# Routed experts in 21 blocks of 128 token slots instead of 14 of 256, with the shared expert's second half as jobs in the same buffers

## What is computed

```
probs = softmax(x @ gate_w.T)                       # 8 experts
routing_weights, selected = top_k(probs, 2)         # normalized to sum 1
out = (silu(x @ shared_gate.T) * (x @ shared_up.T)) @ shared_down.T      # width 704
y_e = (silu(x @ expert_gate[e].T) * (x @ expert_up[e].T)) @ expert_down[e].T   # width 352
out = out + sum over the two selected e of weight_e * y_e
```

## Time and profile before

| | us |
|---|---|
| median of 3 runs | 1053.2 (1052.33 to 1053.86) |
| the profiled execution | 1054.41 |
| its span | 1052.5 |
| mean granted clock of TensorE | 0.982 of 2.4 GHz |

### The profile page before, as it was taken

The page is one execution under the profiler, slowest core; times in us unless marked ns, Lnnn a source line. Parts: engine busy times, 40 slices in busy tenths (PEclk is TensorE's granted clock), DMA queues, the critical chain, the costliest instruction groups (busy, mean ns, idle before and its releaser), DMA issues.

```text
span 1052.5 us, 18925 instructions
## 1 busy us (share of the span) xinstructions
PE 993.0 (94%) x7782; PEld 863.8 (82%) x7782; DVE 540.2 (51%) x1163; ACT 486.8 (46%) x1176; POOL 254.4 (24%) x160
## 2 busy tenths in 40 slices
PE   5999999999999997889999999997897999999998
PEld 4999989899999996667777777775676999999986
DVE  6353535444444444556556556645283555555546
ACT  3351514233233434266666666664332566666631
POOL 1220211202020332020010001002046344434453
PEclk9999999999999998899999999998998999999999
DMA  5110741111010021121010011001047466666545
GB/s 174 62 60 21 237 123 61 42 39 60 21 61 21 21 101 59 50 85 47 21 31 21 12 31 30 12 2 61 31 146 258 187 238 230 234 234 244 195 166 163
DMA packets 41188, 102.50 MB, mean 97 GB/s; under 512 B 3488, under 2 KB 21136, under 8 KB 39184
## 3 DMA queue, kind: packets, MB, share of 16 engines
q1 hardware_dynamic: 38544, 93.97, 26.5%
q0 software_dynamic: 2560, 7.34, 2.1%
HBM read 79.28 MB, written 20.19 MB: 95 GB/s over the span
## 4 chain that ended last, share of the span: by engine, by line
PE 48%; DVE 6%; ACT 2%; POOL 1%; issue 1%; DMA 1%; SPq 0%; ACTq 0%; DVEq 0%
PE bank L444 13%; PE bank L446 12%; PE bank L445 12%; PE bank L641 3%; PE bank L658 3%; PE bank L608 1%; PE bank L759 1%; POOL slots L1831 1%; DVE rq L1397 1%; PE bank L668 1%; DVE kn L1410 0%; DVE yg L1611 0%; PE bank L532 0%; DMA sf<-moe 0%; DVE kT L1419 0%
## 5 line engine op out<-in xcount | busy, mean ns | idle before, releaser
L1736 POOL TENSOR_TENSOR E_lo<-F,E_hi 128x940 fp32r<-128x940 f32 (+1 forms) x28 | 79.9, 2855 | 115.9 <-ACT E_hi L858 115.9
L1018 ACT ACTIVATE ee<-bank 125x448 f32<-125x448 f32 x192 | 91.2, 548 | 23.2 <-PE bank L641 22.2
L444 PE MATMUL bank<-xT_hi,wqk_hi 128*128 128x448 f32 x256 | 96.0, 375 | 1.4 <-DVE xT_lo L1256 1.4
L444 PE MATMUL bank<-xgT_hi,E_hi 128*128 128x256 f32 (+1 forms) x336 | 95.2, 283 | 0.0
L446 PE MATMUL bank<-xgT_lo,E_hi 128*128 128x256 f32 (+1 forms) x336 | 94.7, 282 | 0.0
L445 PE MATMUL bank<-xgT_hi,E_lo 128*128 128x256 f32 (+1 forms) x336 | 94.3, 281 | 0.0
L446 PE MATMUL bank<-xT_lo,wqk_hi 128*128 128x448 f32 x256 | 93.8, 367 | 0.0
L445 PE MATMUL bank<-xT_hi,wqk_lo 128*128 128x448 f32 x256 | 93.8, 366 | 0.0
L444 PE MATMUL bank<-wkv_hi,ctx_hi 128*125 128x512 f32 x192 | 81.5, 424 | 9.6 <-DVE kn L1410 7.8
L1736 POOL TENSOR_TENSOR ctx_lo<-ctx_f,ctx_hi 128x500 fp32r<-128x500 f32 x24 | 29.9, 1246 | 216.1 <-ACT ctx_hi L858 216.1
L445 PE MATMUL bank<-wkv_hi,ctx_lo 128*125 128x512 f32 x192 | 77.1, 402 | 0.0
(11 more groups left out here) (333 smaller groups left out, 2616.2 us busy)
## 6 DMA issues: line engine op xcount, KB each, us to landing
F<-wexp SPq DMA_DIRECT2D x14, 2176.0 KB, 8.5
wqk_f<-wqk SPq DMA_DIRECT2D x16, 512.0 KB, 3.3
slots<-zt SPq DMA_DIRECT2D x1, 7168.0 KB, 29.2
xg<-slots SPq DMA_DIRECT2D x14, 512.0 KB, 3.8
slots_out<-yg SPq DMA_DIRECT2D x28, 256.0 KB, 2.1
sf<-moe SPq DMA_DIRECT2D x9, 768.0 KB
ctx_f<-ctx SPq DMA_DIRECT2D x24, 250.0 KB, 2.7
wv_f<-wv SPq DMA_DIRECT2D x8, 512.0 KB, 3.5
```

The lines of the kernel that those rows point to most:

```text
L444: e.matmul(out, a[0], b[0], start=first, stop=False)
L1018: e.activation(ee[(4 * n + r) % 8][:, :], SX[r][0:MS, 0:4 * T], ACT.Exp, scale=0.25).then_inc(*x_exped.did((n, r)))
L1736: return e.tensor_tensor(out, src, high.bitcast(F32), ALU.subtract)
```

## The change

- BS is 128, so there are 21 routed blocks. They run as jobs in the order s0, e0 to e20, s1, s2. A job s is two chunks of the shared expert's second half, whose weights (2 x 1536 columns) are loaded into the same F and split into the same E as an expert's.
- In a routed job the slots are stationary: 2 (gate, up) x 4 x 3 = 24 matmuls of 352 columns, the weights moving. silu x up comes out with slots on the partitions, so h is turned by 3 transposes into PSUM and split from there by ScalarE and VectorE (384 columns each). The downward product is 9 matmuls of 512 columns and is done during the next job, between or after that job's upward products. x is turned (4 transposes) one job ahead, with two xgT and four xg buffers.
- y is copied out of PSUM by VectorE instead of ScalarE. The low part of the downward piece is made half by VectorE, half by GpSimd (768 columns each).
- The weights come as two DMAs, upward (1408 KB) and downward (768 KB) part, each with a register load of the expert number before it and a semaphore of its own.
- A shared job's downward product sums its two chunks and is added to the output rows by VectorE tile by tile. The last additions of gathered rows: tokens 0 to 447 (additions 0 to 7) after the last split of h, then s2's four tiles, then additions 8 to 15.

The orders of the jobs, cut to their core:

```diff
-BS = 256
+BS = 128
+        jobs = [("s", 0)] + [("e", j) for j in range(NBLK)] + [("s", 1), ("s", 2)]
 # TensorE
+            def expert_up(j, a):
+                for k in range(KC):
+                    i = mm3(GU[u][:, 0:NI], at(xgT[j % 2], ALL, k, ALL), at(p, ALL, toks(k * 2 * NI + a * NI, NI)), k == 0, k == KC - 1)
+            def job_pe(k):
+                kind, j = jobs[k]
...
+                if kind == "e":
+                    expert_up(j, 0)
+                else:
+                    up_pe(1, 2 * j, 0)
+                if prev and prev[0] == "e":
+                    turn_h(prev[1])
+                elif prev and kind == "e":
+                    job_down(*prev)
+                if kind == "s":
+                    up_pe(1, 2 * j, 1)
+                    if k == 0:
+                        up_pe(1, 2 * j + 1, 0)
+                if nxt[0] == "e":
+                    turn_x(nxt[1])
+                if kind == "e":
+                    expert_up(j, 1)
+                if prev and (prev[0] == "e" or kind == "s"):
+                    job_down(*prev)
+                if kind == "s":
+                    if k:
+                        up_pe(1, 2 * j + 1, 0)
+                    up_pe(1, 2 * j + 1, 1)
 # ScalarE, routed job k (part_hi waits for the load's DMA, and for the last reader of E)
+                if kind == "e":
+                    part_hi(k + 1, 0)
+                    if nxt[0] == "e":
+                        part_hi(k + 1, 1)
+                if prev[0] == "e":
+                    ht_hi_act(prev[1])
...
+                if nxt[0] == "e":
+                    turned_hi(nxt[1])
+                if kind == "e":
...
+                    silu(("b", j), ("b", j, 0), (sg1 if j % 2 else sg[0])[:, 0:NI])
+                    if nxt[0] == "e":
+                        part_hi(k + 1, 2)
+                    part_hi(k, 3)
 # VectorE: part_low(k+1,0), ht_low, turned_low, product, part_low(k+1,2), part_low(k,3), y_out(prev)
 # VectorE at the end
+            for n in range(8):
+                add_back(n)
+            y_out(*jobs[-1])
+            for n in range(8, 16):
+                add_back(n)
 # SyncE (part_load(k, p) waits for the low parts of job k - 2 in the same buffer)
+            for k in range(len(jobs)):
+                if k:
+                    part_load(k + 1, 3)
+                part_load(k + 2, 0)
+                if k and jobs[k - 1][0] == "e":
+                    j = jobs[k - 1][1]
+                    w.wait_ge(*y_done["e", j])
+                    e.dma_start(y_d[j * BS:(j + 1) * BS, :], yg[j % 4][:, :]).then_inc(*yo_out[j % 4].did(j))
+                    xg_load(j + 4)
```

## The result

The changed kernel takes 1064.5 us, the median of 4 runs (1063.1 to 1068.1), beside 1053.2 before (1052.3 to 1053.9): ratio 1.0113, 95% interval 1.0086 to 1.0140. Forecast were 1043.7 and faster; it is 11.3 us slower, outside the range of 1020 to 1060. The profiled execution took 1063.1 at a span of 1061.0.

A forecast was written before the change was run, and what follows sets the result against it. TensorE bound the old expert stage; afterwards a loop through SyncE's order would, 2P = 10 + 7.3, 8.65 us per block. With head and tail the span is 1043; 1043 + 1.9 - 1.2 = 1043.7 us, range 1020 to 1060.

The forecast's parts named there:

- a ring through SyncE's wait for y: Expert stage: upward loads are issued only after SyncE's wait for y; the loop passes two jobs, 8.65 us per block.
- I take D+10 for the landing, F: Expert stage: upward weights of job k+3 land (F) 10 us after y of job k's turn is ready (D).
- by landing: Rival, expert stage: weights land at D+11.5, 9.4 us per block, 1057 us in all; chance 14%.
- the head: Before the routed blocks: TensorE's hole shrinks from 6.2 to 2 us without the slow clock; job 2 starts at 824.8.
- the tail: Kernel's end: last gathers wait for additions, last addition at 1039.6, span 1043; about 9 us over TensorE's own end.
- one of my two sums: Landing in the expert stage: by the queue D+9.6, by adding everything to the first issue D+10.2; x and y 1.7.
- F to D: Expert stage: from the weights' landing, ScalarE's 5.6, VectorE's 0.94 and the y copy's 0.69 give the next D at F+7.3.
- TensorE's price: Expert stage: 352-column matmuls at 0.159 us each, 6.7 us per new block, 141 instead of 190.7 us in all.
- Clock: Expert stage: clock stays 1.00; rival, gaps drop it to 1.2 GHz, 95 us more, 1138 us, chance 3%.
- Lock, GpSimd first: Rival, end of each job: GpSimd takes its 768 columns before VectorE, D 1.75 later, 9.5 per block, 1060 us; chance 10%.
- The busiest resource binds, 7.3: Rival, expert stage: loads land sooner or their wait is hidden, 7.3 us per block, 1020 us; chance 16%.
- All are near or above 6.7: Expert stage: ScalarE, VectorE, the VectorE-GpSimd lock and DMA each need near or over TensorE's 6.7 us per block.

The follow-up runs named there:

- experiment 3: Changed kernel with the upward load of job k+2 issued before SyncE's wait for y of job k-2: 1040.2 us, ratio 0.9861 to the kernel before.
- experiment 10: Changed kernel with each routed expert's downward load cut to a quarter of its columns from job 4 on, upward loads whole: 1048.7 us.
- experiments 7 and 12: Changed kernel, from block 4 on, with x loads cut to 64 of 512 columns (1065.4 us), or with y stores cut to 64 of 512 (1066.4 us).
- experiment 9: Experiment 3's kernel with GpSimd's pieces cut to 64 columns from job 4 on: 1036.8 us.
- experiment 8: Changed kernel with eight extra 512-column products on TensorE ahead of each routed job's wait for the low half of h: 1064.9 us.

## Why the prediction was wrong
The mechanism stood in the forecast: a ring through SyncE's wait for y, closed by the landing of the weights. Opening it alone gives back 24 us (experiment 3). **The step that failed is a size: "I take D+10 for the landing, F".** It measures 11.4, and the rival "by landing", D+11.5, given 14%, is what happened in the stage; its time, 1057, is still 7.5 short. By the 10.8 that the lag cost, the forecast would have been 1054.5, an estimate, inside its range: what carried it past 1060 lies in the head and the tail, in which the slow clock was put at nothing, and in 2.8 us around the span. The terms:
- SyncE's issues: first weight load at D+1.8, measured 1.9 to 2.5, mostly 1.9 to 2.0; upward load at about D+3.1. Right.
- From the upward issue to the landing I had 7.0, measured 8.3. The data were priced at 418 GB/s, read from a stretch of 1 us. Single stretches reach that here too (384 to 453), but the difference between loads gives 347 (experiment 10), by which the 2.23 MB of weights take an estimated 1.1 us more. And where one load of 2176 KB landed 8.5 after its issue, two loads of the same bytes take 1.1 + 8.3 = 9.4 from the first issue; what the split into two costs by itself is open, as no run of the changed kernel loads with one. The 1.7 us of x and y that one of my two sums put in front, for which no row was given, cost nothing that the time shows (experiments 7 and 12), which hid part of the error.
- The rule I set aside was nearer: by the Trainium skill's (SBUF — State Buffer, A bandwidth-pool intuition) roughly 358 GB/s from HBM, F would have come an estimated 0.7 to 1 later. Where the DMA engines are full for 60 us they carry 351 to 372 (experiment 9), so a peak of 1 us must not price a load of 7.
- F to D: forecast 7.3, measured 6.95 to 7.73. VectorE's and GpSimd's pieces after the release, ScalarE's order: right.

| | forecast | measured | adds |
|---|---|---|---|
| D of job 3 (second store of y) | 843.9 | 846.3 | 2.4 |
| D of job 19, eight double rounds later | 982.3 | 995.5 | 10.8 |
| last split of h ends | 1024 | 1039.3 | 2.1 |
| last addition ends | 1039.6 | 1058.3 | 3.4 |
| end of the span | 1043 | 1061.0 | -0.7 |

The sum is 18.0. The other 2.8 of the 20.8 lie around the span: its profiled execution was below its median by 1.5, that of before above by 1.2, and 0.1 lies between span and time.
- TensorE's price, 352 columns at 0.159: from 901.10 to 902.70 ten follow each other, 0.16 apart. Right, and worth nothing.
- Head: x at 809.2 forecast, its transposes start at 809.04 after a hole of 2.76; right. But the slow clock, which the forecast left out together with the long hole, came behind the short one too:
```profile
809.04 0.66 PE L784 MATMUL bank<-ident,xg 128*128 128x128 f32 x4 [2.76 <-DMA xg<-slots]
809.97 0.58 PE L475 MATMUL bank<-xT_lo,E_hi 128*128 128x448 f32 x1
```
Until 813.33 nine matmuls of 448 columns are 0.37 apart instead of 0.20, 1.5 us. ScalarE converts job 2's pieces from 821.67 instead of 820 and job 2 starts at 827.08, 2.3 late and again at 1.2 GHz; D of job 2 is 5.2 late, D of job 3 2.4.
- Tail: the additions stand before the last downward tiles as forecast, but these did not end at 1033. TensorE idled 2.05 before the first of them, for the last split, and 3.62 behind the additions; then the clock was at 0.50, the last twelve matmuls came 0.43 apart instead of 0.23, and the last tile came at 1051.6:
```profile
1046.08 0.77 PE L473 MATMUL bank<-E_hi,hs0hi 128*112 128x512 f32 x1 [3.62 <-DVE xs L1605]
1049.21 0.63 PE L474 MATMUL bank<-E_hi,hs0lo 128*112 128x512 f32 x1
```
That is 2.4 of the 3.4 us that the tail adds. Behind it VectorE makes eight additions, six us, without a wait, though the last gather's descriptors were made only at 1051.2: the end was set by VectorE's order and not, as forecast, by the gathers.
- Clock: forecast 1.00 in the stage, measured 0.91 in five of eight stretches. The rival had it in every job, at 95 us; in the stage it was worth an estimated 1 (experiment 8). With the 1.5 of the head and the 2.4 of the tail that is an estimated 5 of the 18 us; the two last are read from rows, no run tests them.
- Lock, GpSimd first: no; VectorE's last piece and the copy of y ran undisturbed in the ring (0.96 at 928.92, 0.68 at 929.80).
- "The busiest resource binds, 7.3": with the ring open it is 7.7 to 7.8 and the DMA engines, not 7.3.
- "All are near or above 6.7" holds for the DMA engines and the lock (7.0 and 7.2), not for ScalarE (5.5 to 6.0) and VectorE (5.6). Nothing rested on it.

At a lag of 11.1 the prediction itself put the break-even; the forecast stood 1.1 us from it, with a landing that could be wrong by 1.5. 57% for it was too much.

## What to carry over
When a change halves the compute per load, look for the ring that now sets the period (which DMA's issue waits for a result that needs that DMA's older data), and write lag + work, divided by the buffers; then move the issue ahead of the wait before doing anything else: here that was worth 24 us. Price a large load by a sustained rate (here about 350, not the 418 of 1 us), from issue to landing, with the loads ahead of it on the same queue; with two buffers each us of error is half a us in every block. A small transfer sent ahead of a large one was free; sent behind it, it inherited the large one's time (x: 3.2 to 8.7 us). And where the change opens a hole in TensorE's work, look at the granted clock behind it and at what waits for those matmuls: the same fall was nearly free in the stage and cost 2.4 us in the tail.

## What the runs showed of the hardware
- Of the 9.5 us around a pair of weight loads about 4.8 are not full flow: in the pair shown 2.7 from the first issue to 384 GB/s and about 2.1 from the flow's end to ScalarE's start. Small stores and loads disappear in it: 0.23 MB less of x or of y left the time as it was.
- A load shares time with the one ahead of it on the queue: 1408 KB land in 8.3 behind 768 KB, 7.2 in front of it, 6.6 behind 192 KB.
- The granted clock dropped to 0.50 (1.2 GHz) behind a hole of 2.3 us (905.7 to 908.0) and was back at 1.00 by 913. A hole's length alone does not decide: of nine holes of 2.27 to 3.05 us from 840 to 1000 five were followed by such a drop (2.31, 2.45, 2.78, 2.83, 3.05) and four were not (2.27, 2.50, 2.59, 3.05).
- VectorE's split of two SBUF operands is stretched from 1.22 to 1.86 on average when GpSimd works beside it, and it returns to 1.28 when GpSimd's pieces are cut (experiments 3 and 9).
